# A two-layer graph network on one core: first layer norm, first projection and the lower triangle of the first dense product done tile by tile inside the attention layer

## The reference

```python
hs = h[src]
e = leaky_relu(score(hs, h[dst], emb_rel[etype]), 0.01)
w = exp(e - segment_max(e, dst)[dst])
agg = segment_sum(w / segment_sum(w, dst)[dst] * hs, dst)        # h itself where a node has no edge
x = layernorm(x + agg + h @ loop_weight)                         # x1 below

for W_r, W_sl, W_el in two_rounds:                               # h starts as x1
    self_msg = where(in_degree == 0, h @ W_el, h @ W_sl)
    agg = segment_sum((rel_embed[etype] + h[src]) @ W_r, dst)
    h = rrelu(agg * deg_isqrt + self_msg)                        # slope 11/48 below zero
x = layernorm(x1 + h)
```

## Time and profile before

| | us |
|---|---|
| median of 3 runs | 3161.61 (3159.47 to 3161.62) |
| profiled execution, its own time | 3161.25 |
| its span in the profile | 3158.8 |
| busy PE, DVE, ACT, POOL | 2275.7, 1917.4, 1093.8, 1590.5 |

### The profile page before, as it was taken

One profiled execution on the slowest core, in us unless ns is written; L12 is line 12 of the kernel. 1 busy time (PEld: TensorE's weight loads), 2 busy tenths in 40 slices (PEclk: granted clock), 3 DMA queues, 4 the chain that ended last, 5 costly groups with the idle time before them and its releaser, 6 DMA issues.

```text
span 3158.8 us, 47055 instructions
## 1 busy us (share of the span) xinstructions
PE 2275.7 (72%) x17758; PEld 1917.1 (61%) x17758; DVE 1917.4 (61%) x3880; ACT 1093.8 (35%) x3267; POOL 1590.5 (50%) x1674
## 2 busy tenths in 40 slices
PE   1566666666666666566666666666899999999999
PEld 1455555555555555556555555553588888788887
DVE  7677777777777777777777777775422222232222
ACT  1344444444444444444444444445311111000000
POOL 4777777777777777777777777770000000000000
PEclk9777787777888777787777787778999999999999
DMA  7545544555555455444445544442255555455554
GB/s 189 164 138 156 156 148 142 149 156 156 156 156 155 140 152 156 155 145 146 149 156 156 156 153 143 150 127 96 82 172 174 169 174 169 153 191 190 191 195 167
DMA packets 166160, 491.65 MB, mean 156 GB/s; under 512 B 78316, under 2 KB 92240, under 8 KB 146105
## 3 DMA queue, kind: packets, MB, share of 16 engines
q1 hardware_dynamic: 110578, 373.50, 34.6%
q0 software_dynamic: 53600, 114.24, 14.8%
q10 hardware_dynamic: 1752, 0.86, 0.1%
HBM read 397.01 MB, written 91.44 MB: 155 GB/s over the span
## 4 chain that ended last, share of the span: by engine, by line
POOL 49%; PE 29%; issue 16%; DVE 3%; ACT 1%; DMA 1%; SPq 0%; ACTq 0%; POOLq 0%; DVEq 0%
POOL arena L462 49%; PE bank L723 26%; PE bank L708 1%; DMA wlp<-n_L_gnn_loop_weight_dram 1%; PE bank L727 1%; DVE arena L1027 1%; PE bank L726 1%; ACT arena L557 0%; DMA arena<-counts 0%; ACT slt L555 0%; PE bank L676 0%; DVE arena L888 0%; DVE tmp L1031 0%; POOL arena L455 0%; ACT nT L547 0%
## 5 line engine op out<-in xcount | busy, mean ns | idle before, releaser
L462 POOL DMA_INDIRECT arena<-rows,srcw x1650 | 1568.5, 951 | 521.9 <-issue 502.4
L723 PE MATMUL bank<-arena 125*125 125x384 bf16 x5000 | 856.1, 327 | 1.8 <-DMA arena<-counts 1.8
L723 PEld LDWEIGHTS bank<-arena 125*125 125x125 bf16 x5000 | 682.2, 137 | 157.2 <-issue 10.1
L888 DVE TENSOR_TENSOR arena<-bank,idx 128x2500 bf16<-128x2500 bf16 x500 | 538.2, 1135 | 120.9 <-PE bank L643 117.5
L676 PE MATMUL bank<-arena 128*125 128x130 f32 x3300 | 500.3, 325 | 104.1 <-ACT arena L523 104.1
L676 PEld LDWEIGHTS bank<-arena 128*125 128x125 f32 x3300 | 492.0, 235 | 107.0 <-issue 104.9
L480 ACT ACTIVATE arena<-bank 128x500 bf16<-128x500 f32 (+3 forms) x960 | 441.3, 537 | 143.8 <-PE bank L614 88.4
L523 ACT ACTIVATE arena<-arena,wexp 128x128 f32<-128x128 bf16 x1650 | 487.5, 388 | 1.6
L622 PE MATMUL bank<-arena 128*128 128x125 bf16 x1650 | 180.4, 309 | 322.4 <-DVE arena L888 322.4
L622 PEld LDWEIGHTS bank<-arena 128*128 128x128 bf16 x1650 | 168.1, 147 | 336.4 <-DVE arena L888 336.4
L643 PE MATMUL bank<-arena 128*128 128x250 bf16 x2500 | 313.6, 271 | 73.1 <-ACT arena L480 56.3
(11 more groups left out here) (219 smaller groups left out, 2092.8 us busy)
## 6 DMA issues: line engine op xcount, KB each, us to landing
arena<-counts SPq DMA_DIRECT2D x200, 781.2 KB, 4.5
counts<-arena SPq DMA_DIRECT2D x50, 1562.5 KB
arena<-dst SPq DMA_DIRECT2D x50, 1056.0 KB
arena<-etype SPq DMA_DIRECT2D x50, 1056.0 KB
arena<-rows,srcw POOLq DMA_INDIRECT x1650
edge_terms<-arena SPq DMA_DIRECT2D x200, 12.4 KB
xt<-in_x_dram SPq DMA_DIRECT2D x50, 62.5 KB
out_dram<-arena SPq DMA_DIRECT2D x50, 62.5 KB
```

What stands on the lines that cost most here:

```text
L462: pool.indirect_dma_start(out=rows[:, q, c, :], out_offset=None, in_=rows0, in_offset=bass.IndirectOffsetOnAxis(ap=srcw[:, q, c:c + 1], ax ...
L723: r = pe.matmul(o, ring[0:TN, m % RD, h % HH, :], hs[k][0:TN, h, :], start=(h == 0), stop=False)
L888: return v.tensor_tensor(hot_.rearrange("p c (j t) -> p c j t", t=2), iotap[:, 0:w].rearrange("p (j t) -> p j t", t=2)[:, None, :, :].broa ...
```

## The change

The middle stage is gone. Each tile is normalised, transposed and projected within its own turn of the attention loop, and at the end of the turn PE multiplies the blocks 0 to t of the tile, from `AT` as it lies in SBUF, by the parts of tiles 0 to t, which exist by then (`row(t)`: t + 1 products and the two for the edge types, into bank 6). DVE adds them to the tile's accumulator in the next turn (`row_sum`). The first dense layer multiplies only the blocks t + 1 to 49 of tiles 0 to 48. The second is as before, with the edge-type counts stored behind the 50 blocks in DRAM and loaded with them.

Bank 6 now belongs to the new steps, so NBK goes from 3 to 2, and the ring of scaled one-hots RING from 17 to 12. Places in SBUF are laid out anew. The square roots are taken per tile. The normalised tile goes to DRAM and comes back for the last layer norm. The load ring has four places of 26 blocks in place of five of 25. The core of the diff:

```diff
-RING = 17
+RING = 12
-NBK = 3
-RD = 5
-HH = HI // 2
+NBK = 2
+RD = 4
+HS = HI + 2
+HH = HS // 2
+for t_ in range(NT - 1):
+    for h_ in range(t_ + 1, HI, HH):
+        PIECES.append((0, t_, h_, min(h_ + HH, HI)))
...
 # SP, at the end of each turn t
+                store_x1(t)
+                store_counts(t)
...
 # ACT
             def types(t):
                 act.wait_ge(s("ct_done"), t + 1)
+                if t >= 2:
+                    act.wait_ge(s("at_stored"), 32 * (t - 1))
+                    act.wait_ge(s("pd0"), t - 1)
...
+            def roots(t):
+                act.wait_ge(s("var"), t + 1)
+                act.activation(nv[0:TN, 1, :], nv[0:TN, 0, :], ACT.Sqrt).then_inc(s("rs1"), 1)
...
                     for j in range(2):
                         batch(t, j)
+                    roots(t)
                     if t + 1 < NT:
                         types(t + 1)
-                    for j in range(2, BT):
-                        batch(t, j)
+                    node_t(t)
+                    batch(t, 2)
+                    node_a(0, t)
+                    batch(t, 3)
+                    node_b(0, t)
+                    batch(t, 4)
...
 # PE
+            def row(t):
+                pe.wait_ge(s("ev"), seq("cnt", t, 3 * BT - 1) + 1)
+                pe.wait_ge(s("h0"), 2 * t + 2)
+                pe.wait_ge(s("hs_ready"), t + 1)
+                o = bank[6][0:TN, 0:ND3]
+                for h in range(t + 1):
+                    pe.matmul(o, AT[0:TN, h, :], hs0[0:TN, h, :], start=(h == 0), stop=False)
+                pe.matmul(o, ctb[:, t % 2, 0, :], relW[:, 0, 0, :], start=False, stop=False)
+                pe.matmul(o, ctb[0:R2, t % 2, 1, :], relW[0:R2, 0, 1, :], start=False, stop=True).then_inc(s("pd0"), 1)
...
                     if t + 1 < NT:
                         types(t + 1)
-                    for j in range(2, BT):
+                    x1_in(t)
+                    batch(t, 2)
+                    x1_node(t)
+                    for j in range(3, BT):
                         batch(t, j)
+                row(t)
...
 # DVE
+                v.tensor_scalar(iso[0:TN, t:t + 1], a[0:TN, D + 1:D + 2], 0.5, None, ALU.is_lt)
+                v.tensor_scalar(niso[0:TN, t:t + 1], a[0:TN, D + 1:D + 2], 0.5, None, ALU.is_ge)
+                v.tensor_scalar(nv[0:TN, 0, 1:2], a[0:TN, D + 2:D + 3], 1.0, None, ALU.max)
...
+                link(v.bn_aggr(mv[0:TN, t, :], stat[0:TN, :]))
+                v.tensor_scalar(nv[0:TN, 0, 0:1], mv[0:TN, t, 1:2], EPS, None, ALU.add).then_inc(s("var"), 1)
...
                 weights(t)
+                if t >= 1:
+                    row_sum(t - 1)
                 if more:
                     prepare_wide(t + 1)
...
                     for j in range(2):
                         batch(t, j)
                     finalize(t)
                     if more:
                         prepare_edges(t + 1)
-                    for j in range(2, BT):
+                    normalise(t)
+                    for j in range(2, 4):
                         batch(t, j)
+                    node_in(0, t)
+                    batch(t, 4)
+                node_out(0, t)
                 if more:
                     terms(t + 1)
```

More of the change, by code:

```diff
@@ L221, in build @@
         kcol_i = carve([P, NGB], I32)
[L222 to L229, removed]
+        here(OHM_AT)
+        ohh = carve([P, NS, NHG], BF16)
+        olt = carve([P, NS, HGR + 2], BF16)
+        here(ROWS_AT)
+        hs1 = carve([P, NT, ND3], BF16)
+        hs = [hs0, hs1]
+        here(HOTB_AT)
+        h1r = carve([P, 4, D])
+        yo = carve([P, 4, D])
+        here(LIST_AT)
         ring = carve([P, RD, HH, TN], BF16)
+        assert at_[0] <= AT_AT
         mv = sb("mv", [P, NT, 2])
@@ L406, in sp_fast @@
                     reshape_terms(t + 1)
[L407 to L422, removed]
+                else:
+                    for m in range(RD):
+                        load_piece(m)
@@ L526, in act_fast @@
                 if t == 0:
+                    roots(0)
                     types(1)
@@ L690, in pe_fast @@
                         batch(0, j)
+                    x1_in(0)
+                    x1_node(0)
                 else:
@@ new lines, in pe_fast @@
+            for m, (k, t, h0, h1) in enumerate(PIECES):
+                job = t if k == 0 else NT - 1 + t
+                first = t + 1 if k == 0 else 0
+                last = HI if k == 0 else HS
+                o = bank[4 + job % 2][0:TN, 0:ND3]
+                if h0 == first and job >= 2:
+                    pe.wait_ge(s("sum_read"), job - 1)
+                pe.wait_ge(s("ring%d" % (m % RD)), 16 * (m // RD + 1))
+                for h in range(h0, h1):
+                    if k == 1 and t == 0:
+                        if h in AMID:
+                            step, tile = AMID[h]
+                            step(tile)
+                        if h < HI:
+                            pe.wait_ge(s("hs_ready"), NT + h + 1)
+                    if h < HI:
+                        r = pe.matmul(o, ring[0:TN, m % RD, h - h0, :], hs[k][0:TN, h, :], start=(h == first), stop=(h == last - 1))
+                    else:
+                        n_ = P if h == HI else R2
+                        r = pe.matmul(o, ring[0:n_, m % RD, h - h0, :], relW[0:n_, k, h - HI, :], start=False, stop=(h == last - 1))
+                r.then_inc(s("piece_done"), 1)
+                if h1 == last:
+                    if k == 0 and t >= 2:
+                        node_t(t - 2)
+                    if k == 0 and t >= 3:
+                        node_m(t - 3)
@@ L1000, in dve_fast @@
                         batch(0, j)
+                    normalise(0)
+                    node_in(0, 0)
                 else:
@@ new lines, in dve_fast @@
+            for t in range(NT + 3):
+                if t < NT:
+                    o = h1r[0:TN, t % 4, :]
+                    if t >= 4:
+                        v.wait_ge(s("hT"), NT + t - 3)
+                    if t < NT - 1:
+                        layer_sum(t, t, o)
+                        v.scalar_tensor_tensor(o, o, SLOPE, o, ALU.mult, ALU.max).then_inc(s("h_ready"), 1)
+                    else:
+                        v.scalar_tensor_tensor(o, acc[0:TN, t, :], SLOPE, acc[0:TN, t, :], ALU.mult, ALU.max).then_inc(s("h_ready"), 1)
+                        v.wait_ge(s("h_ready"), NT)
+                if t >= 3:
+                    node_in(1, t - 3)
+                    node_out(1, t - 3)
```

399 lines of the change are left out of this document (212 added, 187 removed).

## The result

The changed kernel takes 3184.62 us, the median of 5 runs (3180.62 to 3193.35), against 3161.61 for the kernel before in as many runs beside them (3159.47 to 3162.73). The ratio is 1.008, with a 95% interval of 1.0061 to 1.0099: slower by 0.8%, where the prediction had 0.2% faster. The profiled execution took 3191.36 us, 2.0 more than its span of 3189.4.

A forecast was written before the change was run, and what follows sets the result against it. POOL's gathers were taken to bound the attention turns, PE the dense layers. Longer turns +253.1, half clock +33.6, middle stage -71.4 and first dense layer -221.2 gave -5.9: 3155 us against 3161.61, own case 3120 to 3190, 8 in 10 from 3075 to 3215.

The forecast's parts named there:

- From the counts to `row`: Each attention turn, end of edge-type counts to start of `row`: 8.3 us, bounds 7.3 and 9.3, where it was 4.6.
- `row` stands in the open: End of each attention turn: the t + 3 products of `row`, 0.165 us each, are all exposed.
- POOL's pace: Rival, attention turns: POOL's gathers still set the pace of 41.22 us a turn, giving 2869 us; chance 0.04.
- The middle stage's going: From the last turn's first matmul to the first dense product: 110.55 us before, 71.4 us saved.
- the first dense layer: Fewer blocks to multiply after the attention loop: 469.2 us falls to 248.0, saving 221.2.
- short jobs: Last jobs of the first dense layer, 1 to 11 blocks, too short for DVE and ACT: adds 10.6 us.
- The table: ACT's two table loads a turn cost nothing; as a rival, one on the path adds 63 us: 3218 us, chance 0.06.
- The second layer has the same 52 products per tile: Second dense layer: unchanged, costed at nothing.
- The half clock: PE slowed in `row`: 0.7 us a turn, 33.6 in all; as a rival, 1.65 a turn gives 3200 us, chance 0.24.
- my own bound of 0.97 us a turn: Half-clock loss in `row` from which the changed kernel would be slower by over 0.2%.
- 42.45 + 0.165 t: Length in us of attention turn t without half clock; turns 1 to 48 sum to 2231.6, 253.1 more than before.
- the faster start of a turn behind `row`: From L664 to L931's end: 3.77 us in place of 4.58; half the difference taken off each turn.

The follow-up runs named there:

- f1_late: Changed kernel with the edits of e1_order and e2_batch4, and `row(t)` moved into the next turn, ahead of the accumulation: 2862.76 us, 0.9059 of the kernel before.
- f2_both: Changed kernel with the edits of e1_order and e2_batch4 together, `row` left in place: 2989.61 us, 0.9461 of the kernel before.
- e4_noroot: Changed kernel with the square root on ACT replaced by a copy, so no table changes and norms are wrong: 3189.2 us in one run.
- e1_order: Changed kernel with SP issuing the next tile's loads before the output store and reload in the second dense layer: 3159.86 us, 0.9992 of the kernel before.
- f3_short: Changed kernel with `row` cut to one block and the two for the types, other products left out: 2990.66 us in one run.
- f4_banks: Kernel before the change with two PSUM banks in place of three: 3160.72 us, 1.0001 of the kernel before.
- e2_batch4: Changed kernel with DVE making batch 4's one-hots before `node_in` in place of behind it: 3024.34 us, 0.9553 of the kernel before.
- e3_warm: Changed kernel with 14 useless matmuls on PE before batch 4 and 5 before `row`: 3099.02 us, 0.9808 of the kernel before.
- e5_late: Changed kernel with the edits of e1_order and e2_batch4, and `row(t)` moved into the next turn: 4433.51 us on a chip where the kernel before took 4577.73.
- e6_short: Changed kernel with `row` cut to one block and the two for the types: 4566.67 us in one run; kernel before 4577.73 on that chip.
- e7_banks: Kernel before the change with two PSUM banks in place of three: 4612.63 us, 1.0076 of the kernel before on a chip where that took 4577.73.
- e8_both: Changed kernel with the edits of e1_order and e2_batch4 together: 4577.86 us on a chip where the kernel before took 4577.73.

## Why the prediction was wrong

The forecast was 30 us under the median and on the wrong side of no change. That the time still lies between my 3120 and 3190 is luck: two terms were short by 34 and 24.6 us, and two others too dear by 21 and 7. Point by point:

- **What held.** Once the chain is longer than POOL's 41.22, the turn is bound by it: DVE no longer waits for gathers and POOL waits for PE. From the counts to `row` I had 8.3 us, measured 8.27. `row` stands in the open: f1_late, which hides it and moves `row_sum` too, is 135 us below f2_both in the turns, down to POOL's pace. The middle stage's going saved 67.4 us (I had 71.4), and the first dense layer 228.3 (221.2): the last, short jobs cost some 7 where I had 10.6, and the projections a little less than my 0.75 each.
- **The table.** The root's load starts at 1754.78, and DVE uses the root only at 1761.35; the exponential's load ends at 1786.26, 2.1 us before the arguments are there. e4_noroot took 0.06 us a turn off. The Trainium skill (ScalarE: Activation LUTs, "Table sets: the hidden batching unit") warns against just such alternation. Here 98 more loads cost the 48 turns some 3 us together by one run, no more than equal turns differ between runs. Only the last turn shows a cost, 2.7 us. That rival is out.
- **The failed step: "The second layer has the same 52 products per tile", at nothing.** That is true, but the products wait for loads, and these I had not priced. Before, SP's two loads started 3.3 us after a tile's first product (2757.78 against 2754.47) and landed 5.8 us later in the median, into a ring half a tile deeper, and PE waited 1.8 us in all. The change put the reload of the normalised tile ahead of them, made each four percent bigger and the ring shorter. They now start 3.7 us after it in the median, between 1.6 and 4.0, and take 6.3, together more than the 8.5 us that PE needs for a tile, into a ring that holds only two tiles. The stage grew by 24.6 us; e1_order took 29.7 off it (457.4 to 427.7). With that alone mended the kernel is as fast as before (0.9992), so without this loss it would not have been slower. The late loads cost more than the 24.6, since a tile without a wait now takes 8.46 us against 8.58 before. I had looked at SP's queue in the attention layer, where every wait was passed in time, and not at the same queue in the stage that I called unchanged.
- **The half clock, mis-sized.** I had 0.7 us a turn, 33.6 in all; it was 1.40, 67 us. I leaned to the lower bound since an idle of 0.87 before batch 4 had done no harm in tile 48. The idle in the changed kernel was 1.83, and I had written 1.8 down myself; the row nearest to it was product 50, which lost 1.65. It is over my own bound of 0.97 us a turn, from which on my sum says slower.
- **The chain without the clock** came out shorter than 42.45 + 0.165 t, by 0.44 us (2277.4 - 67.2 = 2210.2, against 2231.6), 21 us in all. I had taken only half of the faster start of a turn behind `row`, 0.41 us. Nearly all of it was there: 3.84 us to the arguments, against 4.59 in f3_short, where no long `row` precedes them. That is 0.33 of the 0.44.
- **Small ones.** Turn 1 started 2.5 us late (DVE waited 3.13 us for the gathers; in the other variants on chips of the usual pace it started between 160.1 and 162.6), and the last turn with what follows took 3.9 more than I had; the table loads weigh 2.7 there by e4_noroot, where I had 1.28.

In sum: +2.5, -21 and +34 in the turns, +3.9, -7.2, +24.6, about +36 in the span, 3189.4 against 3152.9. The profiled execution is 6.7 us above the median, which leaves the 30 us. Of the rivals, the half clock came nearest: it took twice what I gave it, which alone would have made my sum 3189, and the second layer, which no rival had, would alone have made it 3180; POOL's pace, to which I gave 0.04 with 2869 us, is right as a price, for a kernel that puts `row` elsewhere.

What stays open: how much of the 24.6 us is the reload ahead of the loads, and how much the bigger pieces or the shorter ring. e1_order shows only that none of it is left once the loads go first. Two banks and the ring of 12 were not taken back in the changed kernel: f4_banks shows two banks to be free only while POOL sets the pace, and the changed kernel's turns are above it. Whether f1_late gains from a third bank was not tried either.

## What to carry to other kernels

A pace set by one engine hides work on another only up to the slack of the chain between them, 4.9 us here, and only at a place where that engine would wait anyway: the same products that cost 188 us at the end of the turn, and 135 at full clock with `row_sum` moved as well, were free between two steps of the next one. Look at a stage that "stays the same" with the queue that feeds it written out anew, since it may have had no slack to begin with. And when a step is put before another on a lightly used engine, ask what PE does in the gap it makes: here two lines swapped on DVE were worth 160 us, 67 of them the clock in `row`.

## What the runs showed of the hardware

- After an idle of 1.83 us on PE, a short batch and one more idle of 0.56, the granted clock was 0.50 for 0.9 to 4.8 us within `row`, in 39 of 48 turns with the same idle times. With the first idle cut to 0.21 (e2_batch4), or filled with matmuls of no use (e3_warm, 19 a turn), it was never 0.50 there.
- Two loads of 812.5 KB took 6.3 us in the median from issue to landing when they went out together, 4.6 in e1_order, where one of the two goes out 4.2 us before the other.
- In turn 35, the table load on ACT began as soon as the instruction before it had ended, while its own activation still waited for its data (1784.98 against 1788.37).
- One chip ran the attention layer of all four kernels profiled there (e5_late, e6_short, e7_banks, e8_both) at 70 to 75 us a turn, with gaps of up to 5.1 us before single matmuls of e8_both that wait for nothing shown, and the dense layers at their usual pace. What makes it so was not found.
